# First layer of a graph network: sum gathered rows of x in three bfloat16 parts, multiply each finished bucket by w1

## The chip, the cores and the metric

The kernel runs on one core of a Trainium2 chip. The metric is device time in microseconds of one execution; lower is better.

## The reference

Two graph layers, each followed by a residual and a layer norm, on 6250 nodes of 256 features and 106250 edges that are sorted by destination:

```python
# first layer
w0_features = x @ w0
w1_features = x @ w1
neighbours = segment_sum(w1_features[src], dst, 6250)
x = layernorm(x + relu(w0_features + neighbours))
# second layer, 8 edge types r, 8 heads of 32
h_all = einsum('nf,rof->rno', x, W)
scores = leaky(h_all[type, src] . attn_src + h_all[type, dst] . attn_dst)
w = softmax of scores over the edges of one dst
x = layernorm(x + segment_sum(h_all[type, src] * w, dst, 6250))
```

## The kernel before, in words

All five engines run instruction lists that are written out by hand; semaphores join them. Nothing is scheduled by a planner: the order of the work is the order of the Python loops.

**Sort (start to about 251 us).** The first layer uses each edge in both directions of a sorted list, so the edges are first put in order of destination bucket. A bucket is 256 nodes, there are BK = 25 of them, and an order for the buckets is chosen by their number of columns; a column is 128 edges of one bucket, and there are 856 (COLS). VectorE does most of it: one-hot masks of buckets (L473, scalar_tensor_tensor over 896 elements, nine of thirteen; ScalarE makes the other four, L1396 to L1399), thirteen running counts (`tensor_tensor_scan`, L546, written to PSUM) each followed by a predicated copy (L538), and from about 101 us thirty steps that move the edges to their places through TensorE matmuls (L1644 `move`, L1656 `settle`; VectorE's L599 to L624). One multiplication on the way is GpSimd's: `jumps` (L1316).

**Products beside the sort.** Meanwhile SyncE loads x transposed (`load_chunk`, L1104), TensorE multiplies each tile of 128 nodes by w1 and w0 side by side (`products`, L1612, 128x512 float32), and ScalarE copies the halves out (`keep_products`): x·w1 through `y_two` (L1384) to the DRAM table `y_d` (L1128), x·w0 (L1385) into the running sums `sums0` in SBUF. Tiles 0 to 5 (EARLY) go before the counts, tiles up to Q_AT = 40 after, the rest between the thirty steps.

**First layer (251 to 1428 us).** For each group of four columns, `gather_columns` (L1303) issues four indirect DMAs on GpSimd, each fetching 128 rows of 256 float32 from `y_d` into a ring of five buffers (RING); ScalarE makes the one-hot selectors `sel0` (`column_one_hots`, L1461 and L1465); TensorE sums (`sum_columns`, L1687): two matmuls 128x128 by 128x256 for each column, one for each half of the bucket; VectorE adds the 512 sums of a column to its bucket (`add_columns`, L777). There are NG = 214 groups. `done_at(t)` is the group after which bucket t is complete, a new one about every 8.9 groups. A complete bucket goes through VectorE (`node_sums` L786 to L796: relu, residual, statistics), GpSimd (`inverse_deviation`, L1326), VectorE (`normalise`, L805), TensorE (`turn_nodes`, L1726, transposes), ScalarE (`copy_nodes`, L1491) and then ten units of the second layer's table (`table_unit` L1737 and L1740, `copy_unit` L1503 to L1512, stored to `ha_d`). turn_at and unit_at say how many groups after done_at these stand. The tables of the second layer's edges are made in the first groups as well (the AT table; GpSimd's L1311 gathers 7 times 128 rows of 512 float32).

**Drain (1428 to 1489 us).** After the last gather the last buckets (22, 23, 24) still go through those stages, and GpSimd waits for the last store to `ha_d`.

**Second layer (from 1489 us)**: 880 gathers from `ha_d` (L1348) with the score and softmax work; then a short tail. Neither is touched, except that a row of indices `tile_row` now shares its buffer with `bucket_row`.

SyncE's loads for the first layer's buckets and for W stand in one queue: W's transpose `WT` comes after the products and the edge rows, and TensorE's list waits for it (`t.wait_ge(wT_in, 16)`) once ahead of group 0.

Of the kernel before, what the change touches and what calls it, by code (L numbers as in the profile page):

```python
# [5 lines left out]
P = 128  # L6
# [15 lines left out]
def graph_layers(nc, x, xT, src, dst, etype, w0, w1, W, WT, attn_src, attn_dst, out):  # L22
# [58 lines left out]
    EARLY = 6  # L81
    GOES_AT, Q_AT = 35, 40
    assert WW <= P and COLS <= KR and OH <= 512 and E <= P * KR and NP_ * 512 < 2 ** 24
    assert WW * HC < HIGH and HIGH * HIGH <= 2 ** 24 and KR < HIGH and NPAIR <= 16
    assert OH % 4 == 0 and OH <= 512 and NT - 1 - Q_AT <= NBT // 2 and 2 * NBT * PP <= P
# [6 lines left out]
    y_d = dram("y_d", [NP_, D], F32)  # L92
# [9 lines left out]
    with ExitStack() as ctx:  # L102
# [7 lines left out]
        RW = 25600  # L110
# [14 lines left out]
        tile_row = sb("tile_row", [1, KP], I32)  # L125
        bucket_row = sb("bucket_row", [1, KR], I32)
        wab = sb("wab", [P, DC, 2 * RH], F32)
# [49 lines left out]
        def view16(base, at, *shape):  # L177
# [22 lines left out]
        cells_i = view(region, RW - COLS, COLS).bitcast(I32)  # L200
        assert GA + NPAIR * KR // 2 <= RW - COLS
        win = [view16(region, GA, TB, WW)] + [view16(region, GA + TB * WW // 2 * n, TB // 2, WW, 2) for n in range(1, 4)]
        at = [view16(region, GA + 2 * TB * WW + TB * HC * n, 2, TB // 2, HC, 2) for n in range(3)]
        iota_h = view16(region, RW - COLS - COLS // 2, COLS)
        assert GA + 2 * TB * WW + 3 * TB * HC + KR <= RW - COLS - COLS // 2
# [3 lines left out]
        w01 = view(edge_z, o, DC, 2 * D); o += 2 * DC * D  # L209
        x_t = [view(edge_z, o + 2 * DC * P * n, DC, 2 * P) for n in range(2)]; o += 4 * DC * P  # L210
        y_two = [view(edge_z, o + 2 * D * n, 2, D) for n in range(2)]; o += 4 * D
        misc = view(nodes, NT * D, NT * H)
        assert o <= 4864
# [47 lines left out]
        assert 2 * R * AW <= 4 * D * RING  # L261
        rows0 = [view(region, o + 4 * D * n, 4, D) for n in range(RING)]; o += 4 * D * RING
        sel0 = [view(region, o + 4 * SPAN * n, 4, SPAN) for n in range(SEL)]; o += 4 * SPAN * SEL
# [3 lines left out]
        xn = [view(edge_z, o + 2 * D * h, 2, D) for h in range(2)]; o += 4 * D  # L267
        tmp = [view(edge_z, o + 2 * D * h, 2, D) for h in range(2)]; o += 4 * D
# [60 lines left out]
        names = """pads_set edges_in acol_in w_in iotas setup sort_ps sort_in y_ps y_done y_kept bt_made masked counted v_made  # L329
            goes_made cells_made scans summed wp_made split_made grids_made at_made at_filled win_v win_a moved halves_made s_near s_made  # L330
# [59 lines left out]
        def y_tile_at(k):  # L390

            return Q_AT + k // 2 + 1 if k % 2 and Q_AT + k // 2 + 1 < NT else None
# [19 lines left out]
        def turn_at(t):  # L412

            return done_at(t) + (9 if t < BK - 1 else 13)
# [4 lines left out]
        def unit_at(t, k):  # L419

            return done_at(t) + (10 if t < BK - 1 else 19) + 9 * k // 10
# [1464 lines left out]
```

## Time and profile before

| what | us |
|---|---|
| median of 3 runs | 2759.0 (2754.98 to 2760.86) |
| profiled execution, its own time | 2753.04 |
| its span, first to last instruction | 2751.2 |
| TensorE, VectorE, ScalarE, GpSimd busy | 2309.0, 1940.0, 1637.1, 1841.7 |
| granted TensorE clock, mean | 0.902 |

The span is 1.8 us shorter than the execution's time. In the rows below PE is TensorE, PEld its weight loads, DVE VectorE, ACT ScalarE and POOL GpSimd. A busy share is a mean over four stages with different limits, so the rows are taken stage by stage.

### The profile page before, as it was taken

Reading aid. Unit: us, or ns where it says so; the run is one execution under the profiler, and the core shown is the slowest. Engines: PE = TensorE matmul, PEld = TensorE weight load, DVE = VectorE, ACT = ScalarE, POOL = GpSimd, SP = SyncE. Lnnn points to the kernel's source line nnn. Section 1 sums busy time; section 2 is a strip of 40 time slices with the busy share of each in tenths; the row PEclk is TensorE's granted clock in tenths of the full one; section 3 lists DMA queues with packets and bytes.
Section 4 is the critical chain, followed back from the end, with each engine's and each line's share of the span. In section 5 each row is a group of like instructions: output and inputs, shape, how many; then the busy total and the mean of one; then the engine's idle time right before and its main releaser. Section 6 shows DMA issues by size and latency. Waiting matters only on the chain. (4 is left out here: it accounts for less than half of the span.)

```text
span 2751.2 us, 38107 instructions
## 1 busy us (share of the span) xinstructions
PE 2309.0 (84%) x9936; PEld 1645.4 (60%) x9936; DVE 1940.0 (71%) x4273; ACT 1637.1 (60%) x3465; POOL 1841.7 (67%) x1875
## 2 busy tenths in 40 slices
PE   8796788999999999999987677777778878787775
PEld 3364666677777777777764555555555555555541
DVE  9895576555555555555552688888888888888887
ACT  4563455566666666666654566666666666666643
POOL 1002677777777777777762777777777777777735
PEclk9797899999999999999998698889888887889888
DMA  5202346764444444444464444554454445454535
GB/s 158 62 22 86 109 133 140 224 195 160 154 161 152 161 148 147 158 153 163 153 137 160 138 138 138 142 146 138 138 144 145 138 138 149 139 139 138 143 90 159
DMA packets 177777, 387.53 MB, mean 141 GB/s; under 512 B 42669, under 2 KB 106867, under 8 KB 171042
## 3 DMA queue, kind: packets, MB, share of 16 engines
q0 software_dynamic: 83888, 233.09, 30.4%
q1 hardware_dynamic: 86626, 99.05, 12.0%
q10 hardware_dynamic: 7056, 52.99, 4.9%
q8 instruction: 86, 1.41, 0.2%
q14 instruction: 121, 0.99, 0.1%
HBM read 302.96 MB, written 82.03 MB: 140 GB/s over the span
## 5 line engine op out<-in xcount | busy, mean ns | idle before, releaser
L1303 POOL DMA_INDIRECT region<-y_d,edge_z x856 | 875.2, 1022 | 472.1 <-issue 235.1
L1348 POOL DMA_INDIRECT region<-ha_d,idx_t x880 | 892.5, 1014 | 310.8 <-issue 228.9
L777 DVE TENSOR_TENSOR nodes<-ps,nodes 128x512 f32 x856 | 591.7, 691 | 501.8 <-PE ps L1687 384.7
L1687 PE MATMUL ps<-region 128*128 128x256 f32 x3424 | 795.0, 385 | 75.4 <-DMA region<-y_d,edge_z 22.9
L1687 PEld LDWEIGHTS ps<-region 128*128 128x128 f32 x3424 | 651.2, 193 | 250.6 <-issue 122.6
L1803 PE MATMUL ps<-region 128*128 128x264 f32 x1760 | 623.6, 485 | 160.0 <-DVE nodes L895 118.9
L1803 PEld LDWEIGHTS ps<-region 128*128 128x128 f32 x1760 | 350.9, 226 | 358.0 <-DVE nodes L895 239.4
L895 DVE TENSOR_TENSOR nodes<-ps,nodes 128x264 f32 x880 | 372.2, 423 | 54.2 <-DVE nodes L895 43.5
L1461 ACT ACTIVATE region<-iota_n,edge_z 128x256 f32<-128x256 f32 x856 | 364.7, 499 | 52.9 <-PE ps L1687 48.9
L1737 PE MATMUL ps<-region,edge_z 128*128 128x512 f32 x784 | 363.0, 592 | 4.0 <-ACT edge_z L1491 2.7
L1503 ACT COPY region<-ps 128x512 f32<-128x512 f32 x196 | 114.6, 586 | 341.6 <-PE ps L1737 290.8
L1786 PEld LDWEIGHTS ps<-edge_z,region 128*128 128x128 f32 x1760 | 258.5, 219 | 66.6 <-issue 51.6
L1556 ACT ACTIVATE region<-region,ones 128x512 f32<-128x512 f32 x220 | 158.8, 722 | 233.0 <-PE ps L1803 227.8
L1786 PE MATMUL ps<-edge_z,region 128*128 x1760 | 262.5, 300 | 28.9 <-issue 19.1
L1549 ACT ACTIVATE region<-iota_row,local_t 128x128 f32<-128x128 f32 x880 | 277.6, 386 | 0.0
L884 DVE TENSOR_TENSOR region<-region,ps 128x1024 f32<-128x1024 f32 x220 | 265.1, 1205 | 0.0
L1465 ACT ACTIVATE region<-region,ones 128x1024 f32<-128x1024 f32 x214 | 246.0, 1150 | 7.0
L1737 PEld LDWEIGHTS ps<-region,edge_z 128*128 128x128 f32 x784 | 146.9, 189 | 125.3 <-issue 114.0
L1542 ACT ACTIVATE region<-region,part 128x512 f32<-128x512 bf16 x220 | 155.4, 706 | 22.8 <-PE ps L1786 14.9
L1545 ACT ACTIVATE region<-region,ones 128x512 f32<-128x512 f32 x220 | 158.8, 722 | 7.1
L938 DVE TENSOR_TENSOR region<-region 128x128 f32<-128x128 f32 x55 | 16.1, 293 | 156.4 <-DMA region<-ha_d,idx_t 156.4
L1820 PE MATMUL ps<-ident,region 128*128 128x128 f32 x55 | 25.1, 457 | 93.7 <-DVE region L940 93.7
(265 smaller groups left out, 1857.6 us busy)
## 6 DMA issues: line engine op xcount, KB each, us to landing
ha_d<-region ACTq DMA_DIRECT2D x49, 1056.0 KB
region<-near_d SPq DMA_DIRECT2D x55, 512.0 KB, 5.4
region<-ha_d,idx_t POOLq DMA_INDIRECT x880, 2.9
region<-y_d,edge_z POOLq DMA_INDIRECT x856, 2.9
edge_z<-level_d SPq DMA_DIRECT2D x55, 136.0 KB, 3.7
kl_d<-region SPq DMA_DIRECT2D x8, 903.0 KB
edge_z<-kl_d SPq DMA_DIRECT2D x55, 129.0 KB, 2.7
y_d<-edge_z SPq DMA_DIRECT2D x25, 256.0 KB, 3.2
```

Source lines behind the costliest of these rows:

```text
L777: v.tensor_tensor(into, ps[:, u, :], into, ALU.add).then_inc(added0, 1)
L884: v.tensor_tensor(rows[s][:, 4 * q:4 * q + 4, 0:D].rearrange("p u (h d) -> p u h d", h=H), rows[s][:, 4 * q:4 * q + 4, 0:D].rearrange("p u ...
L895: v.tensor_tensor(acc[:, ds(tile * AW, AW)], ps[:, u, 0:AW], acc[:, ds(tile * AW, AW)], ALU.add).then_inc(added, 1)
L1303: g.indirect_dma_start(rows0[c % RING][:, u, :], None, y_d, bass.IndirectOffsetOnAxis(ap=y_idx[:, k:k + 1], axis=0), bounds_check=node_bou ...
L1348: g.indirect_dma_start(rows[s][:, k, :], None, ha_rows, bass.IndirectOffsetOnAxis(ap=idx_t[:, B * b + k:B * b + k + 1], axis=0), bounds_ch ...
L1461: last = a.activation(sel0[c % SEL][:, u, :], iota_n[:, :], ACT.Abs, bias=y_local[:, 4 * c + u:4 * c + u + 1], scale=-1.0)
L1465: a.activation(sel0[c % SEL].rearrange("p u n -> p (u n)"), sel0[c % SEL].rearrange("p u n -> p (u n)"), ACT.Relu, bias=ones[:, 0:1], scal ...
L1549: last = a.activation(apart[q % 2][:, u, :], iota_row[:, :], ACT.Abs, bias=local_t[:, ds(B * b + 4 * q + u, 1)], scale=-1.0)
L1687: mm = t.matmul(ps[:, u, h * D:(h + 1) * D], lhsT=sel0[c % SEL][:, u, h * P:(h + 1) * P], rhs=rows0[c % RING][:, u, :], start=True, stop=True)
L1737: mm = t.matmul(ps[:, 4 + n % 2, :], lhsT=xts[par][:, h, c, :], rhs=wT_sb[:, c, 512 * q:512 * q + 512], start=(c == 0), stop=(c == DC - 1))
L1786: mm = t.matmul(ps[:, 5 + q // 2, at_col:at_col + RH], lhsT=st[q][:, u, :], rhs=b_sb[:, ds(tile[u] * RH, RH)], start=True, stop=True)
L1803: t.matmul(ps[:, u, 0:AW], lhsT=sel[q][:, u, :], rhs=rows[b % 4][:, 4 * q + u, :], start=True, stop=True).then_inc(segs, 1)
```

## The change

**The table of products goes.** No `products`, no `keep_products`, no `y_d`. Instead each chunk of x (12 of 128 partitions by 4 rows of 256, and one of 106 rows) is split into three bfloat16 parts whose sum is x: ScalarE rounds (`round_high`), GpSimd subtracts in place (`take_high`), ScalarE rounds the rest (`round_rest`), GpSimd subtracts again into the third part (`take_mid`), SyncE stores the three parts (`store_chunk`) to `x3_d`. Four chunks are in flight (HELD). GpSimd then sets `sums0` to zero (128x12800).

**The gather** fetches rows of 768 bfloat16 instead of 256 float32, and a column is summed by six bfloat16 matmuls (three parts, two halves), accumulated in PSUM; the selectors are bfloat16.

**A finished bucket** has four stages more ahead of `node_sums`: `turn_sums` (TensorE, 4 transposes), `copy_sums` (ScalarE), `node_products` (TensorE: 4 matmuls of x by w0 and 4 of the sums by w1, into one bank of PSUM), and SyncE loads the bucket's columns of x transposed (`load_columns`). `turn_at` and `unit_at` are one group earlier (three for bucket 23 and 24). TensorE's wait for WT moves from ahead of group 0 to the first table unit.

```diff
+            def take_high(k):
+                p, t = chunk_of(k)
+                g.wait_ge(x_high, k + 1)
+                g.tensor_tensor(x_in[k % HELD][p, t, :], x_in[k % HELD][p, t, :], x_parts[k % HELD][p, t, 0, :],
+                                ALU.subtract).then_inc(x_rest, 1)
+
+            def take_mid(k):
+                p, t = chunk_of(k)
+                g.wait_ge(x_mid, k + 1)
+                g.tensor_tensor(x_parts[k % HELD][p, t, 2, :], x_in[k % HELD][p, t, :], x_parts[k % HELD][p, t, 1, :],
+                                ALU.subtract).then_inc(x_low, 1)
+
+            take_high(0)
+            for k in range(CHUNKS):
+                if k + 1 < CHUNKS:
+                    take_high(k + 1)
+                take_mid(k)
+                if k == JUMPS_AT:
+                    g.wait_ge(goes_made, 1)
+                    g.tensor_tensor(jumps, ...)
+            for n in range(HELD):
+                g.wait_ge(x_stored[n], 16 * chunks_in(n))
+            g.memset(sums0, 0.0).then_inc(sums_zero, 1)
...
-            def keep_products(tile):
+            def round_high(k):
+                a.wait_ge(x_loaded[k % HELD], 16 * (k // HELD + 1))
+                if k >= HELD:
+                    a.wait_ge(x_stored[k % HELD], 16 * (k // HELD))
+                a.copy(x_parts[k % HELD][p, t, 0, :], x_in[k % HELD][p, t, :]).then_inc(x_high, 1)
+            def round_rest(k):
+                a.wait_ge(x_rest, k + 1)
+                a.copy(x_parts[k % HELD][p, t, 1, :], x_in[k % HELD][p, t, :]).then_inc(x_mid, 1)
...
-                    g.indirect_dma_start(rows0[c % RING][:, u, :], None, y_d,
+                    g.indirect_dma_start(rows0[c % RING][:, u, :], None, x3_d,
...
-                        mm = t.matmul(ps[:, u, h * D:(h + 1) * D], lhsT=sel0[c % SEL][:, u, h * P:(h + 1) * P],
-                                      rhs=rows0[c % RING][:, u, :], start=True, stop=True)
+                        for k in range(PARTS):
+                            mm = t.matmul(ps[:, u, h * D:(h + 1) * D], lhsT=sel0[c % SEL][:, u, h * P:(h + 1) * P],
+                                          rhs=rows0[c % RING][:, u, k * D:(k + 1) * D], start=(k == 0), stop=(k == PARTS - 1))
...
+            def node_products(job):
+                for h in range(2):
+                    for c in range(DC):
+                        t.matmul(ps[:, 7, h * D:(h + 1) * D], lhsT=x_t[par][:, c, h * P:(h + 1) * P],
+                                 rhs=w01[:, c, D:2 * D], start=(c == 0), stop=False)
+                    for c in range(DC):
+                        mm = t.matmul(ps[:, 7, h * D:(h + 1) * D], lhsT=sums_t[par][:, h, c, :],
+                                      rhs=w01[:, c, 0:D], start=False, stop=(c == DC - 1))
...
-            t.wait_ge(wT_in, 16)
```

Where the instructions moved, GpSimd's list from its start to the first gather. `nodes` is the buffer that holds the chunks of x and their parts, `region` holds `jumps`. Before:

```order
L1292 ISA
L1292 IOTA region 128x896
L1293 IOTA nodes 128x1
L1316 TENSOR_TENSOR region<-region 128x2600
L1303 DMA region<-y_d,edge_z 128x256 x64
```

Now, to the first of the alternating subtractions:

```order
L1333 ISA
L1333 IOTA region 128x896
L1334 IOTA nodes 128x1
L1359 TENSOR_TENSOR nodes<-nodes 128x1024 x2
L1365 TENSOR_TENSOR nodes<-nodes 128x4x256
L1359 TENSOR_TENSOR nodes<-nodes 128x1024
```

GpSimd did one multiplication before the first gather. Now L1359 and L1365 go on in turn to 24 subtractions of 1024 elements and two of 256; `jumps` (now L1375) stands behind the sixth L1365, and the memset of `sums0` and the gathers behind the last.

TensorE's list around the last sum of columns, where the drain begins. Before, L1687 is that sum, L1726 `turn_nodes`, L1737 and L1740 table units:

```order
L1737 MATMUL ps<-region,edge_z 128x512 x2
L1687 MATMUL ps<-region 128x256 x8
L1740 MATMUL ps<-wab,edge_z 128x128 x2
L1726 MATMUL ps<-ident,edge_z 128x128 x4
L1737 MATMUL ps<-region,edge_z 128x512 x8
```

Now, L1740 is the sum, L1823 and L1826 are units, L1782 `turn_sums`, L1794 and L1797 `node_products`:

```order
L1740 MATMUL ps<-region 128x256 x24
L1823 MATMUL ps<-region,edge_z 128x512 x6
L1782 MATMUL ps<-ident,nodes 128x128 x4
L1823 MATMUL ps<-region,edge_z 128x512 x2
L1794 MATMUL ps<-region,edge_z 128x256 x2
L1797 MATMUL ps<-region,edge_z 128x256 x2
```

The products of bucket 23, and behind them those of bucket 24, stand between the units of bucket 22; the transposes L1726 of bucket 22 moved ahead of the last sum.

## Rows read from the trace of the kernel before

**Rows 1.** Windows of the stages: busy us (instructions) of each engine, clock, DMA share.
```profile
core 0: us, PE busy (x) PEld busy (x) DVE busy (x) ACT busy (x) POOL busy (x), PEclk, DMA share, GB/s
0.00:251.00 251.00, 203.91 (x1317) 119.93 (x1317) 220.72 (x359) 131.97 (x357) 8.32 (x8) 0.87 0.23 66
251.00:1428.00 1177.00, 1101.12 (x4449) 821.46 (x4450) 676.60 (x1106) 721.28 (x1365) 898.87 (x886) 0.97 0.51 158
1428.00:1489.00 61.00, 50.68 (x160) 26.93 (x158) 24.00 (x32) 19.32 (x43) 2.31 (x3) 0.98 0.41 131
```
**Rows 2.** Line L1303, the gathers: idle time of GpSimd before them, by releaser.
```profile
  issue: 235.1, 777
  DVE edge_z L661: 196.8, 1
  PE ps L1687: 40.2, 78
```
**Rows 3.** Groups of GpSimd, 251 to 1489 us: busy us, mean ns | idle us before.
```profile
L1326 POOL TENSOR_TENSOR rstd<-veps,minus_half 128x2 f32<-128x2 f32 x25 | 18.8, 750 | 16.5 <-DVE veps L796 16.0
L1311 POOL DMA_INDIRECT region<-edge_rows_d,nodes x7 | 7.1, 1012 | 2.1 <-issue 2.1
```
**Rows 4.** Timeline of GpSimd: start, us, instruction [idle before <-releaser].
```profile
47.01 6.97 POOL L1316 TENSOR_TENSOR region<-region 128x2600 f32<-128x2600 f32 x1 [45.20 <-DVE region L551]
297.35 1.01 POOL L1303 DMA_INDIRECT region<-y_d,edge_z  x1 [9.74 <-PE ps L1687]
298.67 1.01 POOL L1303 DMA_INDIRECT region<-y_d,edge_z  x1 [0.30 <-issue]
318.26 1.01 POOL L1303 DMA_INDIRECT region<-y_d,edge_z  x1 [5.13 <-PE ps L1687]
```
**Rows 5.** Timeline of VectorE around GpSimd's multiplication, and its memset in the drain.
```profile
46.84 2.09 DVE L546 TENSOR_TENSOR_SCAN ps<-ones,region 128x896 f32<-128x896 f32 x1
48.84 1.17 DVE L538 COPY_PREDICATED region<-region,ps 128x896 f32<-128x896 int16 x1
50.04 5.83 DVE L546 TENSOR_TENSOR_SCAN ps<-ones,region 128x896 f32<-128x896 f32 x1
...
1449.22 11.06 DVE L846 MEMSET nodes<- 128x13200 f32 x1 [2.70 <-DMA x_d<-edge_z]
```
**Rows 6.** Groups of VectorE in the sort, 0 to 251 us.
```profile
L546 DVE TENSOR_TENSOR_SCAN ps<-ones,region 128x896 f32<-128x896 f32 x13 | 30.7, 2368 | 0.2
L617 DVE TENSOR_SCALAR region<-region 104x856 f16<-104x856 f16 x60 | 23.7, 436 | 10.6 <-PE ps L1656 10.2
L624 DVE TENSOR_TENSOR region<-ps,region 104x512 f16<-104x512 f32 x30 | 20.5, 682 | 5.4 <-PE ps L1644 5.4
L473 DVE SCALAR_TENSOR_TENSOR region<-region 128x896 bf16<-128x896 f32 x9 | 9.2, 1089 | 0.0
L465 DVE CAST region<-region 128x896 f32<-128x896 int32 x1 | 0.6, 628 | 0.0
```
**Rows 7.** ScalarE, page, costliest groups: one pass over 1024 elements.
```profile
L1465 ACT ACTIVATE region<-region,ones 128x1024 f32<-128x1024 f32 x214 | 246.0, 1150 | 7.0
```
**Rows 8.** Timeline of TensorE: a product and a `settle` in the sort, then the later stages.
```profile
119.02 3.10 PE L1612 MATMUL ps<-edge_z 128*128 128x512 f32 x4
...
232.18 1.63 PE L1656 MATMUL ps<-region 104*128 104x428 f16 x8
...
269.96 9.68 PE L1687 MATMUL ps<-region 128*128 128x256 f32 x32 [21.07 <-DMA region<-WT_in]
...
1430.55 3.73 PE L1687 MATMUL ps<-region 128*128 128x256 f32 x16 [1.20 <-DMA region<-y_d,edge_z]
...
1439.56 0.61 PE L1740 MATMUL ps<-wab,edge_z 128*128 128x128 f32 x4
1440.01 0.60 PE L1726 MATMUL ps<-ident,edge_z 128*128 128x128 f32 x4
...
1450.00 7.11 PE L1737 MATMUL ps<-region,edge_z 128*128 128x512 f32 x16 [0.32 <-ACT region L1503]
```

More of the change, by code:

```diff
@@ L349, in graph_layers @@
         xt_in = [sem(f"xt_in{h}") for h in range(2)]
-        y_stored = [sem(f"y_stored{h}") for h in range(2)]
         x1_kept = [sem(f"x1_kept{h}") for h in range(2)]
@@ L808, in _ @@
             pad_rows()
-            v.wait_ge(jobs_made, 1)
-            job_regs = [v.alloc_register(f"sum_job{k}") for k in range(BK - 1)]
-            v.load(job_regs, job_row[0:1, 0:BK - 1])
-            jobs = [v.snap(r, min_val=0, max_val=BK - 2) for r in job_regs] + [BK - 1]
             for g in range(NG + LATE):
@@ L1400, in _ @@
                              accum_out=cnt_all[:, t:t + 1]).then_inc(counted, 1)
-                keep_products(k + 1)
-            for tile in range(NPAIR - MASKED + 1, EARLY):
-                keep_products(tile)
+                split_chunk(k)
             a.wait_ge(sort_ps, PS["v"])
@@ L1408, in _ @@
                        ps[:, 4 + n, 0:(blocks.stop - blocks.start) * P].rearrange("p (b t) -> p b t", t=P)).then_inc(sort_in, 1)
-            for tile in range(EARLY, Q_AT + 1):
-                keep_products(tile)
-                if tile == GOES_AT:
+            for k in range(NPAIR - MASKED, CHUNKS):
+                split_chunk(k)
+                if k == GOES_AT:
                     a.wait_ge(sort_ps, PS["goes"])
@@ L1442, in _ @@
                     windows_of(ahead, TBG // 2 * (k % 4), TBG // 2 * (k % 4) + TBG // 2)
-                if y_tile_at(k) is not None:
-                    keep_products(y_tile_at(k))
                 if k == 2:
@@ L1601, in turn_rows @@
                 return mm
-            t.wait_ge(w_in, 32)
-            def products(tile):
-                it, h = tile // 2, tile % 2
-                if h == 0:
-                    t.wait_ge(xt_in[it % 2], 16 * (it // 2 + 1))
-                if tile >= 2:
-                    t.wait_ge(y_done, tile - 1)
-                for c in range(DC):
-                    mm = t.matmul(ps[:, tile % 2, :], lhsT=x_t[it % 2][:, c, h * P:(h + 1) * P], rhs=w01[:, c, :],
-                                  start=(c == 0), stop=(c == DC - 1))
-                mm.then_inc(y_ps, 1)
-            for tile in range(EARLY):
-                products(tile)
             t.wait_ge(counted, NPAIR - MASKED + 1)
@@ L1624, in _ @@
             turn_rows(v_row, 4).then_inc(sort_ps, 1)
-            for tile in range(EARLY, Q_AT + 1):
-                products(tile)
-                if tile == GOES_AT:
-                    t.wait_ge(goes_made, 3)
-                    t.transpose(ps[0:WW, 7, P:2 * P], goes_row, ident[:, :]).then_inc(sort_ps, 1)
+            t.wait_ge(goes_made, 3)
+            t.transpose(ps[0:WW, 7, P:2 * P], goes_row, ident[:, :]).then_inc(sort_ps, 1)
             t.wait_ge(summed, NPAIR + 2)
@@ L1664, in _ @@
                     settle(k - 1)
-                if y_tile_at(k) is not None:
-                    products(y_tile_at(k))
                 if k == 1:
@@ L1755, in _ @@
                 for job in range(BK):
+                    if c == sums_at(job):
+                        turn_sums(job)
+                    if c == sums_at(job) + 1:
+                        node_products(job)
                     if c == turn_at(job):
```

226 lines of the change are left out of this document (147 added, 79 removed).

## The prediction

> **What bounds the kernel now.** I read the windows of the stages first, then for each stage the engine that is never idle in it.
>
> In the **sort** that is VectorE: 220.7 of 251 us busy [rows 1]. GpSimd stands idle for 196.8 us there, until the sorted indices are out [rows 2]. So whatever lengthens VectorE's chain delays the first gather one for one.
>
> In the **first layer** it is GpSimd. A gather takes 1.01 us and the next starts 1.32 us after it (298.67 against 297.35) [rows 4]; 856 of them are 1130 us of the stage's 1177 [rows 1]. Of the rest, 26 us are the 25 small powers (18.8 us) and the seven gathers of table rows (7.1) [rows 3]. Only 40.2 us in 78 pieces is waiting for TensorE [rows 2], and most pieces are as long as the pause that any gather has (235.1/777 = 0.30 us), so the true loss is 40.2 - 78 x 0.30 = **16.8 us**, nearly all in two places, 9.74 and 5.13 us [rows 4]. TensorE looks just as busy, 1101 of 1177 us, and DMA has half its share free (0.51) [rows 1].
>
> In the **drain** it is TensorE, 50.7 of 61 us [rows 1].
>
> **The change, part by part, on the path.** All sums are made against the profiled execution's 2753.0 us.
>
> *1. Subtractions beside the sort.* GpSimd gets 24 subtractions of 1024 elements and two of 256. The nearest row is its multiplication of 2600 elements, 6.97 us from 47.01 [rows 4]. A scan on VectorE ran from 46.84 to 48.93 [rows 5]. If GpSimd began only behind it, the work took 53.98 - 48.93 = 5.05 us, 1.94 ns an element; if it began at once, 2.68 ns. A subtraction is thus 2.0 or 2.7 us, and I take 2.0, because the other engine's row says who waited: the next scan, started at 50.04, took 5.83 us instead of 2.09 and ended 1.9 us after the multiplication did, so it began when that was over. The predicated copy between them took its usual 1.17 [rows 5, 6]. A scan has two operands in SBUF (ones and masks), the copy has its data in PSUM. **I conclude that a VectorE instruction with two SBUF operands and a GpSimd operation of this kind exclude each other.**
>
> The masks (L473, 1.09 us for 896 elements, two SBUF operands) are the scan's kind. The casts (0.63 us) have one operand but take 0.70 ns an element where the masks take 1.2, so I count them as using the second path too; if they do not, 7 us less.
>
> Stepping the hand-written lists with 2.0 us a subtraction, 1.15 us for a ScalarE rounding [rows 7] and the rows of VectorE: (a) from 14 us on, nine subtractions alternate with the nine masks, and each holds the next mask for most of its 2.0 us: 16 us. (b) Three fall among short operations, many with no second SBUF operand: 3.5 us. (c) The other twelve run beside the thirteen scans. Where one starts as a scan ends, the copy (1.17) goes on beside it and the next scan waits 0.85 us: nine of them, 7.6 us. Three stand ahead of casts or of another two-operand instruction at 2.0: 6 us. Sum 16 + 3.5 + 7.6 + 6 = **+33 us**. Lower bound, if scans alone are held: 12 x 0.85 = 10. Upper, at 2.7 us each: 33 + 24 x 0.74 = 51. I take 33. The subtractions end some 115 us into the kernel, well before the gathers need them, so the split itself is hidden; the price is VectorE's.
>
> The page SBUF — State Buffer of the Trainium skill, section Who interferes with whom, says the same of two-SBUF-input instructions against a GpSimd instruction that reads SBUF, and of casts that use both ports; by it the sum is the 33. It speaks against placing this work on GpSimd beside a VectorE-bound sort, and the scan's row agrees with it. The page GPSIMD Engine Reference, section 3.1, gives 4497 ns for a float32 tensor_tensor of 2048; an estimate from that page is 2.3 us a subtraction, by which the term would be about 40.
>
> *2. Zeroing `sums0`.* 12800 elements on GpSimd; VectorE's memset of 13200 took 11.1 us [rows 5]. It comes once the last part is stored, when VectorE still runs scans, and 130 us before the first gather. No row shows a GpSimd memset beside VectorE: between 0 and +11; I take 0, as GpSimd's idle 196.8 us covers it and the copy's row shows that operations without a second operand pass.
>
> *3. Products leave the sort.* In the thirty steps VectorE waits 10.2 + 5.4 us for TensorE [rows 6], partly behind products of up to 3.1 us [rows 8]. The rest is TensorE's own moves, which stay. Bounds 0 and -15.6; I take half, **-8 us**.
>
> *4. Start of the first layer.* TensorE's first sum is held to 269.96 by WT [rows 8]; that wait moves away, and TensorE starts some 10 us earlier, as soon as rows and selectors are there. GpSimd's two long waits at 297 and 318 follow from that late start, so they go: **-16.5 us**, the most that GpSimd's row allows. Bounds: 0 and -16.8.
>
> *5. Rows of 1536 bytes.* A gather of 2048-byte rows took 1012 ns, like one of 1024 [rows 3]: 0 on GpSimd. Gathered bytes grow by half; DMA's share would go from 0.51 to at most 0.75. 0 to +20 us in case landings get late; I take 0.
>
> *6. TensorE's steady load.* For each bucket (8.9 groups, 8.9 x 4 x 1.32 = 47.0 us of GpSimd) it had sums of 8.9 x 3.73 = 33.2 us, units 2 x (7.11 + 0.61) = 15.4, transposes 0.6 [rows 8]: 49.2, a little over what the overlapped records really cost. Now: bfloat16 columns are priced by the f16 row, 1.63/8 for 428 columns, 0.122 us for 256; 24 in a group make 2.9, 26.0 for 8.9 groups; units 15.4; 16 product instructions at 3.73/16 make 3.7; two sets of transposes 1.2: 46.3. That is 2.9 less than by the same pricing before, so GpSimd stays the bound: 0.
>
> *7. Drain.* Behind the last sum TensorE gets two sets of products (2 x 3.7) and two of `turn_sums` (1.2), loses one set of transposes and the wait for its copy (0.6 + 1.5), has a last sum of 2.9 instead of 3.7 us and one hop of about 1 that nothing covers: 8.6 - 2.1 - 0.8 + 1 = 6.7, of which some 2.5 replaces waits between units: **+4 us**; bounds 0 and +9.
>
> **Sum:** 33 - 8 - 16.5 + 4 = +12.5, so 2765.5 on the profiled execution. That one lies 6 us under the median of the runs shown, so the forecast is **2772 us**.
>
> **Rivals.** *A: only scans are held.* Then term 1 is 10, VectorE loses little, and 10 - 8 - 16.5 + 4 = -10.5: 2749 us, faster. For it: the scan's is the only stall the rows show. Against: the masks have the same two operands. It decides in the masks, at 14 to 24 us: if they still end by 26, it is so. *B: subtractions cost 2.7 us.* Term 1 is 51: 2790. For it: 6.97 us is what the row says; against: the scan that was running when it began. *C: the first layer gets a new bound* (late landings, or bfloat16 matmuls no quicker than f16 rows say): 10 to 20 us more, some 2790. *D: the change does not do what it says*: if a 256-column bfloat16 matmul costs what a float32 pass does (3.73/16 = 0.23), a group is 24 x 0.23 = 5.6 us and a bucket 5.6 x 8.9 + 20.3 = 70 against 47: over 500 us slower. The f16 row speaks against it, at 0.20 us for 428 columns.
>
> **How the numbers follow.** The forecast 0.48, A 0.25, B 0.15, C 0.10, D 0.02. About 0.2% (5.5 us) is what a measurement here can tell from no change. The forecast's own terms spread from 2757 (casts not held, all of term 3) to 2785 (nothing of term 3, a drain of +9), so it gives some 0.10 to "same"; A reaches into it too. Faster 0.25, same 0.13, slower 0.62. The range goes from A with all of term 3 gained, 2742, to B with most of the memset's 11 us, 2798.
>
> **What would show it.** Right: masks that end near 40 us instead of 24; scans of 2.8 to 4 us where a subtraction of about 2.0 us runs; the first gather near 275 instead of 251; GpSimd hardly waiting for TensorE between the first and the last gather, about 1160 us apart; a drain of about 65 us. Wrong: masks back to back beside subtractions (A); subtractions of 2.7 us (B); gathers that wait for TensorE in mid-stage, or sums that wait for rows (C, D); or a second layer that changes, which no step touches.

## The result, and the profile after

The changed kernel takes **2789.3 us** (median of 4 runs, 2787.9 to 2790.5) against 2758.0 (4 runs, one more than ahead of the prediction, 2755.0 to 2760.9): ratio 1.0109, 95% interval 1.0096 to 1.0123, or 31 us slower. The profiled execution took 2790.5 us with a span of 2788.7, that is 37.5 more than the span of before. (The profiled execution of before lies 5 us under its median, this one 1 above; that is the rest.)

Windows of the stages after, columns as in [rows 1]:

```profile
core 0: us, PE busy (x) PEld busy (x) DVE busy (x) ACT busy (x) POOL busy (x), PEclk, DMA share, GB/s
0.00:280.00 280.00, 120.54 (x1117) 86.48 (x1117) 258.27 (x357) 124.80 (x283) 88.68 (x34) 0.91 0.21 70
280.00:1456.00 1176.00, 1061.52 (x6599) 754.85 (x6599) 675.42 (x1106) 726.39 (x1387) 900.00 (x886) 0.95 0.68 211
1456.00:1523.00 67.00, 57.77 (x223) 33.69 (x220) 25.28 (x34) 21.41 (x47) 1.42 (x3) 0.95 0.41 134
1523.00:2788.00 1265.00, 946.70 (x4012) 674.73 (x4012) 1018.52 (x2779) 764.54 (x1700) 936.30 (x980) 0.84 0.49 140
```

The sort holds almost all of it: 280 us instead of 251, with VectorE busy for 258 instead of 221 on nearly the same instructions (357 and 359). The first layer is as long as before. Measured between the starts of fixed instructions, in us (the rank phase is the running counts and what follows them up to a cast, L569 before and L593 now; then the first and the last gather of the first layer, and the first of the second):

| stretch | before | after | difference |
|---|---|---|---|
| start to the end of the rank phase | 94.1 | 130.3 | +36.2 |
| to the first gather | 156.7 | 149.9 | -6.8 |
| first to last gather | 1175.9 | 1174.8 | -1.1 |
| drain | 61.9 | 68.4 | +6.5 |
| second layer | 1262.6 | 1265.3 | +2.7 |

The last line is scatter: in the kernels below, none of which touches the second layer, it takes 1261.8 to 1266.0. Each figure is from one traced execution, and the others scatter too. From the rank phase to the first gather the code of before took 153.9 to 157.9 us in three executions, that of after 146.8 to 156.0 in seven (means 156.2 and 150.5). The drain took 61.6 to 61.9 in the former three, and 65.9 to 69.9 in all ten executions that have the change's four stages.

**The sort.** Groups of VectorE, 0 to 131 us, which answer to [rows 6], and of GpSimd, 0 to 281 us:

```profile
L570 DVE TENSOR_TENSOR_SCAN ps<-ones,region 128x896 f32<-128x896 f32 x13 | 36.6, 2823 | 0.2
L562 DVE COPY_PREDICATED region<-region,ps 128x896 f32<-128x896 int16 x13 | 14.9, 1145 | 0.1
L497 DVE SCALAR_TENSOR_TENSOR region<-region 128x896 bf16<-128x896 f32 x9 | 22.5, 2559 | 0.0
L590 DVE CAST region<-region 128x896 int32<-128x896 f32 x1 | 4.3, 4305 | 0.0
```

```profile
L1359 POOL TENSOR_TENSOR nodes<-nodes 128x1024 f32<-128x1024 f32 x12 | 34.7, 2893 | 7.6 <-ACT nodes L1444 7.6
L1365 POOL TENSOR_TENSOR nodes<-nodes 128x1024 bf16<-128x1024 f32 x12 | 33.8, 2820 | 12.5 <-ACT nodes L1449 12.5
```

A mask takes 2.56 us instead of 1.09, a scan 2.82 instead of 2.37; the predicated copy keeps its 1.15. VectorE's idle time up to the end of the rank phase does not grow (4.6 us, against 6.8 before): the wait for the other engine is inside the instruction's own record. So it is on GpSimd's side. Its timeline, and VectorE's, with the cast of before to compare:

```profile
19.52 2.97 POOL L1365 TENSOR_TENSOR nodes<-nodes 128x1024 bf16<-128x1024 f32 x1
...
85.77 3.84 POOL L1365 TENSOR_TENSOR nodes<-nodes 128x1024 bf16<-128x1024 f32 x1
89.57 2.12 POOL L1359 TENSOR_TENSOR nodes<-nodes 128x1024 f32<-128x1024 f32 x1
...
117.25 10.77 POOL L1379 MEMSET nodes<- 128x12800 f32 x1 [6.84 <-DMA x_d<-nodes]
```

```profile
15.14 2.43 DVE L495 CAST region<-region 128x896 f32<-128x896 int32 x1
...
20.44 3.00 DVE L497 SCALAR_TENSOR_TENSOR region<-region 128x896 bf16<-128x896 f32 x1
...
91.73 3.95 DVE L570 TENSOR_TENSOR_SCAN ps<-ones,region 128x896 f32<-128x896 f32 x1
...
119.75 2.09 DVE L570 TENSOR_TENSOR_SCAN ps<-ones,region 128x896 f32<-128x896 f32 x1
121.75 2.41 DVE L562 COPY_PREDICATED region<-region,ps 128x896 f32<-128x896 int16 x2
124.19 4.30 DVE L590 CAST region<-region 128x896 int32<-128x896 f32 x1
```

```profile
91.70 0.63 DVE L566 CAST region<-region 128x896 int32<-128x896 f32 x1
```

Beside seven of the nine masks the two engines alternate, with a period of 2.93 us on both: one mask (the next starts 1.01 us later where nothing holds it) and one subtraction (some 1.9). A subtraction that nothing holds takes 2.12; one that meets a scan reads 3.84. A cast is held as well (2.43 us at 15.14, 0.63 by itself). The memset, which reads nothing, lets a scan pass (2.09), but the cast behind it, L590, ends only 0.5 us after the memset does at 128.0. So the 36.2 us of the rank phase are 32.5 ahead of L590 (124.19 against 91.70) and 3.7 in it (4.30 against 0.63).

**The first layer.** GpSimd's first gather and its long waits, to be set against [rows 4]:

```profile
280.19 1.30 POOL L1344 DMA_INDIRECT region<-x_d,edge_z  x1 [152.18 <-DVE edge_z L685]
321.77 1.01 POOL L1344 DMA_INDIRECT region<-x_d,edge_z  x1 [4.65 <-PE ps L1740]
342.73 1.01 POOL L1344 DMA_INDIRECT region<-x_d,edge_z  x1 [5.08 <-PE ps L1740]
...
379.36 0.73 POOL L1386 TENSOR_TENSOR rstd<-veps,minus_half 128x2 f32<-128x2 f32 x1 [4.77 <-DVE veps L821]
```

The wait of 9.74 has halved, that of 5.13 is still there, and a new one of 4.77 stands behind them: the power (`inverse_deviation`) keeps its place seven groups after `done_at`, but `node_sums`, on which it waits, went from one group after `done_at` to three. TensorE's rows of the same stretch and of the drain, one of ScalarE, and three of TensorE before (two of the first layer, one of the drain) say where the rest comes from:

```profile
291.11 4.59 PE L1740 MATMUL ps<-region 128*128 128x256 bf16 x24 [12.21 <-DMA region<-x_d,edge_z]
297.62 4.48 PE L1740 MATMUL ps<-region 128*128 128x256 bf16 x24 [1.92 <-DMA region<-x_d,edge_z]
301.93 2.75 PE L1750 MATMUL ps<-nodes,edge_z 128*128 128x16 f32 x24
...
305.76 5.28 PE L1750 MATMUL ps<-nodes,edge_z 128*128 128x16 f32 x24
...
316.22 11.02 PE L1740 MATMUL ps<-region 128*128 128x256 bf16 x72 [3.46 <-issue]
...
1465.26 4.47 PE L1740 MATMUL ps<-region 128*128 128x256 bf16 x24 [2.80 <-DMA region<-x_d,edge_z]
```

```profile
312.79 0.21 ACT L1538 COPY wab<-ps 128x64 f32<-128x64 f32 x1 [22.92 <-PE ps L1750]
```

```profile
279.47 2.75 PE L1697 MATMUL ps<-nodes,edge_z 128*128 128x16 f32 x24
...
282.96 3.16 PE L1697 MATMUL ps<-nodes,edge_z 128*128 128x16 f32 x24
...
1435.99 3.73 PE L1687 MATMUL ps<-region 128*128 128x256 f32 x16
```

L1750 are the **small weights**: W times the attention vectors, 32 matmuls (64 records) that TensorE does once, behind the second sum of columns. ScalarE copies their result behind its second selectors, so it waits 22.92 us for them and starts no third selectors until 313.2; the third sum comes at 316.22. The block is in the kernel before at the same place (L1697, 279.47 to 287.82 us there). Its two halves are of equal length in work, yet the second takes 5.28 us against 2.75: the granted clock fell from its upper to its lower level meanwhile, and its mean over the block is 0.64, against 0.85 in the kernel before.

### The profile page after: what moved, and what is told of

Its sections match the earlier page's. It is cut to its first block and busy times, and to the rows that moved or that the text cites. A ratio compares the mean times of both kernels' runs of the same rounds, so it can differ in the third digit from the quotient of the medians.

```text
span 2788.7 us, 42188 instructions
## 1 busy us (share of the span) xinstructions
PE 2186.5 (78%) x11948; PEld 1549.8 (56%) x11948; DVE 1977.5 (71%) x4273; ACT 1637.2 (59%) x3416; POOL 1926.4 (69%) x1902
## 5 line engine op out<-in xcount | busy, mean ns | idle before, releaser
L1344 POOL DMA_INDIRECT region<-x_d,edge_z x856 | 876.2, 1024 | 419.0 <-issue 238.1
L1740 PE MATMUL ps<-region 128*128 128x256 bf16 x5136 | 655.8, 285 | 111.9 <-DMA region<-x_d,edge_z 63.8
L1892 PE MATMUL ps<-region 128*128 128x264 f32 x1760 | 617.4, 481 | 160.6 <-DVE nodes L916 120.3
L1740 PEld LDWEIGHTS ps<-region 128*128 128x128 bf16 x5136 | 513.4, 102 | 289.2 <-issue 112.2
L1892 PEld LDWEIGHTS ps<-region 128*128 128x128 f32 x1760 | 347.0, 224 | 356.3 <-DVE nodes L916 238.9
L1527 ACT ACTIVATE region<-iota_n,edge_z 128x256 bf16<-128x256 f32 x856 | 364.8, 500 | 40.1 <-PE ps L1740 34.0
L1823 PE MATMUL ps<-region,edge_z 128*128 128x512 f32 x784 | 365.2, 594 | 3.1 <-ACT region L1575 3.1
L1875 PEld LDWEIGHTS ps<-edge_z,region 128*128 128x128 f32 x1760 | 261.2, 221 | 66.9 <-issue 52.0
L1531 ACT ACTIVATE region<-region,ones 128x1024 bf16<-128x1024 bf16 x214 | 245.8, 1148 | 7.0
L1823 PEld LDWEIGHTS ps<-region,edge_z 128*128 128x128 f32 x784 | 137.0, 191 | 117.7 <-issue 115.4
```

What stands on the lines that cost most here:

```text
L1344: g.indirect_dma_start(rows0[c % RING][:, u, :], None, x3_d, bass.IndirectOffsetOnAxis(ap=y_idx[:, k:k + 1], axis=0), bounds_check=node_bo ...
L1527: last = a.activation(sel0[c % SEL][:, u, :], iota_n[:, :], ACT.Abs, bias=y_local[:, 4 * c + u:4 * c + u + 1], scale=-1.0)
L1531: a.activation(sel0[c % SEL].rearrange("p u n -> p (u n)"), sel0[c % SEL].rearrange("p u n -> p (u n)"), ACT.Relu, bias=ones[:, 0:1], scal ...
L1740: mm = t.matmul(ps[:, u, h * D:(h + 1) * D], lhsT=sel0[c % SEL][:, u, h * P:(h + 1) * P], rhs=rows0[c % RING][:, u, k * D:(k + 1) * D], st ...
L1823: mm = t.matmul(ps[:, 4 + n % 2, :], lhsT=xts[par][:, h, c, :], rhs=wT_sb[:, c, 512 * q:512 * q + 512], start=(c == 0), stop=(c == DC - 1))
L1875: mm = t.matmul(ps[:, 5 + q // 2, at_col:at_col + RH], lhsT=st[q][:, u, :], rhs=b_sb[:, ds(tile[u] * RH, RH)], start=True, stop=True)
```

## The experiments

Each kernel was timed against the kernel before on the same chip. All ratios are to that kernel; the changed kernel's is 1.0109 (1.0096 to 1.0123), and 0.001 is 2.8 us.

**What the subtractions cost** (`e1_narrow`)

```diff
+            for n in range(HELD):
+                g.memset(x_parts[n][:, :, 2, :], 0.0)
-                g.tensor_tensor(x_in[..][p, t, :], x_in[..][p, t, :], x_parts[..][p, t, 0, :], ...
+                g.tensor_tensor(x_in[..][p, t, 0:16], x_in[..][p, t, 0:16], x_parts[..][p, t, 0, 0:16], ...
```

(and the same in `take_mid`)

> Left out: GpSimd's subtractions work on 16 of every 256 columns of x (the third parts are set to zero once at the start), so the second and third parts are wrong. All 26 subtractions, their waits, ScalarE's roundings and SyncE's loads and stores stay. Theory: VectorE's chain is 36.2 us later than before (130.95 against 94.78) because each subtraction of 2.1 us holds VectorE's two-operand instructions. Then masks end by about 27 us instead of 40, scans take 2.1 to 2.6 us again, the chain ends at about 97 to 100, and the whole gains 30 to 34 us (about 2757). Rival: the chain is late because of ScalarE, which rounds between its own masks, or of the loads of x; then masks still end near 40 and the time stays within 5 us of 2789.

Measured: 2753.7 us, ratio 0.9990 (0.9980 to 1.0000). The rank phase ends at 96.8 instead of 130.3, the first gather comes at 245.2. VectorE's groups of this run, 0 to 131 us:

```profile
L570 DVE TENSOR_TENSOR_SCAN ps<-ones,region 128x896 f32<-128x896 f32 x13 | 30.6, 2363 | 0.2
...
L497 DVE SCALAR_TENSOR_TENSOR region<-region 128x896 bf16<-128x896 f32 x9 | 9.7, 1138 | 0.0
```

The cast L590 of this run:

```profile
94.06 0.95 DVE L590 CAST region<-region 128x896 int32<-128x896 f32 x1
```

ScalarE's roundings and SyncE's transfers are all still there, so the rival is out: the width of GpSimd's operands alone moves the end of the chain by 33.5 us. Of these, 30.1 lie ahead of the cast (124.19 against 94.06). The other 3.4 are the cast's: in this run the chain reaches it just as the memset ends (94.5), and it takes 0.95.

**The memset** (`e3_small_memset`)

```diff
+            g.memset(sums0[:, HELD * ROWS * D * 5 // 2:], 0.0)
             take_high(0)
...
-            g.memset(sums0, 0.0).then_inc(sums_zero, 1)
+            g.memset(sums0[:, 0:64], 0.0).then_inc(sums_zero, 1)
```

> Left out: sums0 is not zeroed but for its first 64 elements at the old place and its last 2560 at the very start, so the first layer's sums start from what the buffer held. Theory: the memset of 10.8 us holds VectorE's casts (one took 4.30 us instead of 0.63 until the memset's end), so without it the chain from the rank phase to the first gather is 3.7 us shorter: first gather at about 276.5, time about 2785. Rival: the casts only moved the wait, and VectorE then waits for TensorE or ScalarE in the thirty steps: first gather stays at 280, time within 1 us of 2789.

Measured: 2783.0 us, ratio 1.0092 (1.0074 to 1.0110); the interval overlaps that of the changed kernel, so the time decides nothing. In the trace the cast is back to its own length and the rank phase ends 2.6 us earlier (127.7):

```profile
125.26 0.63 DVE L590 CAST region<-region 128x896 int32<-128x896 f32 x1
```

The first gather still came at 281.6: the thirty steps took 4 us longer in this execution, at a clock of 0.73 to 0.86 in their later windows. The chain had reached the cast 1.1 us later than in the changed kernel, so the rank phase gained 2.6 and not the 3.7 that the cast gave back. So the hold is shown, and its price at the first gather is not.

**The wait for WT** (`e2_wt_ahead`, `e6_before_wt_moved`): put back in the changed kernel, moved alone in the kernel before.

```diff
+            t.wait_ge(wT_in, 16)
             unit = 0
```

> TensorE's wait for WT is put back ahead of group 0. Theory A (as predicted): the wait is what makes GpSimd lose its two long waits of 9.7 and 5.1 us in the first layer, and something new took the gain; then putting it back costs 12 to 17 us (2801 to 2806). Theory B: GpSimd's long waits follow from the small weights L1750, which hold TensorE for 11 us and ScalarE's selectors for 23 us just behind the second sum; the wait for WT only shifts when that block begins, by some 8 us less the slower clock of the block. Then it costs 4 to 6 us (2793 to 2795) and GpSimd waits 9 to 10 us near 327 and still 5 us some 20 us later. Theory C: the wait is hidden: within 2 us of 2789.

Measured: 2797.3 us, ratio 1.0149 (1.0133 to 1.0165), some 11 us more than the change by the two ratios; first to last gather 1182.6 against 1174.8. GpSimd waits 10.91 us at 327 and 4.19 at 347. Between B and A by the time, at B by the trace.

```diff
-            t.wait_ge(wT_in, 16)
             unit = 0
...
+                if n == 0:
+                    t.wait_ge(wT_in, 16)
```

> The kernel before with one part of the change alone: TensorE's wait for WT goes from ahead of group 0 to the first table unit. The prediction took 16.5 us for it. Theory B, from the run that put the wait back (first layer 1182.6 against 1174.8): 6 to 9 us, so 2748 to 2751, with the wait of 9.7 us at 297 about halved and the one of 5.1 us still there. Rival: in the kernel before it hides a wait that the change has removed, and gives 14 us or more (2743 or less).

Measured: 2749.5 us, ratio 0.9966 (0.9953 to 0.9978), 9.4 us faster; first to last gather 1171.6 against 1176.0, with waits of 2.91, 4.87 and 2.89. So the wait is worth 4 to 8 us in the first layer of either kernel and 9 to 11 by the ratios, and not the 16.5 that were forecast. The rival's 14 is out.

**The small weights** (`e4_weights_early`, `e5_weights_ahead`)

```diff
             for k in range(NBT):
                 move(k)
                 if k:
                     settle(k - 1)
+                if 10 <= k < 10 + DC * R:
+                    small_weights(k - 10)
```

> The small weights (L1750 and ScalarE's copies L1538 and L1539) leave the first layer: TensorE does them in 16 pieces beside steps 10 to 25 of the sort, ScalarE copies them ahead of its first selectors. Theory B: then neither TensorE nor ScalarE stops behind the second sum, GpSimd's wait at 321 (4.65 us) goes, the first wait of a gather comes later and is shorter, and the time falls by 4 to 9 us (2780 to 2785). Theory A or C: the waits come from late rows (WT and the edge rows share the DMA queues in the first 20 us) or from VectorE's table work, so GpSimd waits as long as before and the time stays within 2 us of 2789. If the pieces delay the thirty steps, the first gather comes after 280.

Measured: 2782.9 us, ratio 1.0102 (1.0087 to 1.0118): no measurable gain. But the parts moved far: first to last gather 1161.7 instead of 1174.8, and from the rank phase to the first gather 159.6 instead of 149.9. VectorE's waits in the steps, of the changed kernel and of this one:

```profile
DVE region L641 <- PE ps L1712: 3.8, 4, 1.6
```

```profile
DVE region L641 <- PE ps L1711: 13.7, 10, 2.4
```

TensorE's pieces, 0.6 us each, were not free there: VectorE waits for `settle` ten times instead of four. So the block goes where TensorE idles, in the 12 us before the first rows land:

```diff
+            small_weights()
             unit = 0
             for c in range(NG + LATE):
                 if c < NG:
                     sum_columns(c)
-                if c == AT["wab"]:
-                    small_weights()
...
-                if c == AT["wab"]:
+                if c == SEL - 1:
                     small_weights()
```

> In the changed kernel, TensorE does the small weights in one block between the last settle of the sort and the first sum, where it waited 12 us for the first rows; ScalarE copies them behind its third selectors instead of its second. In the run that did them beside the thirty steps the first layer fell from 1174.8 to 1161.7 us but the steps grew by 10. Theory B: the block at the start is what cost the first layer its 13 us and the steps only lost TensorE time; here both are saved: first layer about 1162, steps as in the changed kernel (147 to 150), time 2772 to 2777. Rival: the gain came from a warm TensorE clock or from gathers that started later, not from the block; then the first layer stays at 1172 to 1176 and the time at 2785 to 2789.

Measured: 2775.3 us, ratio 1.0067 (1.0054 to 1.0080), 11.6 us faster than the change; first to last gather 1160.6, the steps as they were (148.9). TensorE's rows:

```profile
277.69 2.79 PE L1750 MATMUL ps<-nodes,edge_z 128*128 128x16 f32 x24
...
282.03 5.28 PE L1750 MATMUL ps<-nodes,edge_z 128*128 128x16 f32 x24
...
289.60 4.89 PE L1740 MATMUL ps<-region 128*128 128x256 bf16 x24 [0.58 <-DMA region<-x_d,edge_z]
296.49 10.12 PE L1740 MATMUL ps<-region 128*128 128x256 bf16 x72 [2.01 <-DMA region<-x_d,edge_z]
```

The third sum follows the second without a break, and GpSimd's waits for TensorE, of the changed kernel and of this one, become the pause that any gather has:

```profile
POOL region L1344 <- PE ps L1740: 28.7, 66, 5.1
```

```profile
POOL region L1344 <- PE ps L1740: 16.7, 57, 0.3
```

The power's wait of 4.77 is gone too, though `node_sums` stands where the change put it; one of 3.45 us at 619 is the only wait of GpSimd over 0.8 us that is left in the stage. TensorE's block and ScalarE's copies moved together here, so which of the two held the third sum is not separated; nor did a run move the block and keep WT's wait. And the block fell to the lower clock level here as well (0.51 in the window from 280 to 290 us), straight behind the last `settle`, with no wait of TensorE in front of it.

**The wide rows** (`e10_one_part`, `e11_ahead_one_part`)

```diff
-                    g.indirect_dma_start(rows0[c % RING][:, u, :], None, x3_d, ...
+                    g.indirect_dma_start(rows0[c % RING][:, u, 0:D], None, x3_d, ...
...
-                                          rhs=rows0[c % RING][:, u, k * D:(k + 1) * D], ...
+                                          rhs=rows0[c % RING][:, u, 0:D], ...
```

> Left out: the changed kernel gathers only the first part of each row, 512 bytes instead of 1536, and sums that part three times, so the work of TensorE is the same and the output lacks two parts. Theory (wide rows are hidden, as predicted): the first layer stays at 1172 to 1177 us and the time at 2785 to 2790; only the drain, where the last sum waited 2.8 us for rows, gets 2 to 4 us shorter. Rival: late rows in the first 20 us (the first sum came 11 us after the first gather) are what keeps the first layer from gaining: then the first sum comes 2 us or more earlier and the first layer falls by 4 us or more.

Measured: 2775.5 us, ratio 1.0069 (1.0049 to 1.0090): 11 us faster, against the theory. First to last gather 1164.2. But the drain stayed at 68.3, and the first sum came only 1 us earlier (10.0 us after the first gather instead of 10.9), so the rival is not right as it was put either. What differs in this trace is the clock. TensorE's rows, and the window 300 to 310 us of the changed kernel and of this one:

```profile
290.39 5.15 PE L1740 MATMUL ps<-region 128*128 128x256 bf16 x24 [11.25 <-DMA region<-x_d,edge_z]
297.45 2.80 PE L1740 MATMUL ps<-region 128*128 128x256 bf16 x24 [1.90 <-DMA region<-x_d,edge_z]
300.09 2.75 PE L1750 MATMUL ps<-nodes,edge_z 128*128 128x16 f32 x24
...
303.58 3.53 PE L1750 MATMUL ps<-nodes,edge_z 128*128 128x16 f32 x24
...
312.27 10.05 PE L1740 MATMUL ps<-region 128*128 128x256 bf16 x72 [3.46 <-issue]
```

```profile
300.00:310.00 10.00, 10.00 (x64) 9.48 (x62) 2.05 (x3) 0.00 (x0) 7.60 (x8) 0.67 0.54 165
```

```profile
300.00:310.00 10.00, 8.81 (x67) 8.71 (x64) 1.41 (x3) 1.15 (x6) 7.56 (x9) 0.78 0.16 48
```

The second sum takes 2.80 us here and 4.48 there, the block of small weights 8.7 (mean clock 0.81) against 10.8 (0.64), and the third sum comes 4 us earlier. Whether the narrower rows brought the higher clock is not shown: the block took 8.35 to 11.2 us in the six kernels that keep it at its place with wide or float32 rows. And the third sum is not the whole gain. Of the 10.6 us of the stage, 6.2 are idle time of GpSimd (269.6 us between its instructions instead of 275.8) and 4.4 are its instructions' own records (894.3 instead of 898.7). The same edit on top of `e5_weights_ahead`:

> Left out: as in the run with one part, only the first 512 bytes of each row are gathered and summed three times; and the small weights stand ahead of the first sum, as in the run that took 2775.3 us. Theory: the wide rows cost the changed kernel 11 us only because they keep TensorE waiting and its clock low where the block of small weights holds up the first groups; without the block on that path the narrow rows gain little: first layer 1158 to 1162 us, time 2771 to 2776. Rival: wide rows cost about 10 us on their own, over the whole first layer (GpSimd's issues, late rows, VectorE's stages): then the first layer falls to about 1150 and the time to 2763 to 2767.

Measured: 2770.2 us, ratio 1.0043 (1.0029 to 1.0057); first to last gather 1157.0 against 1160.6. With the block out of the way the narrow rows give 3.6 us in the first layer instead of 10.6 (6.6 by the ratios, in intervals that overlap). Stage and time lie just under the theory's ranges and above the rival's. So 4 (by the ratios) to 7 (by the traces) of the 11 hang on the block, and 4 to 7 are the rows' own. Of the 3.6 in the layer, 2.1 are idle time of GpSimd (262.1 instead of 264.2), 1.6 its own records (894.7 instead of 896.3).

**Versions that beat both kernels** (`e7_before_weights_ahead`, `e8_split_on_tensor`, `e9_split_ahead`). The first is the kernel before with the WT wait moved (as above) and the small weights ahead of the first sum (as above), and nothing of the change's split.

> The kernel before with the wait for WT moved and the small weights ahead of the first sum, that is without the change's split and its four stages. Theory B: the first layer loses nothing to TensorE, 1160 to 1163 us instead of 1176, so 2741 to 2745. Rival: float32 sums of 3.7 us a group leave TensorE too little room in the first groups and GpSimd waits again: 1168 us or more, 2749 or more.

Measured: 2743.2 us, ratio 0.9942 (0.9929 to 0.9955); first to last gather 1164.1.

The second keeps the change, has the small weights ahead of the first sum, and takes the subtractions from GpSimd. TensorE forms x minus its parts in PSUM, ScalarE rounds from there and zeroes `sums0` (operands shortened):

```diff
-            def take_high(k): ...
-            def take_mid(k): ...
-            g.memset(sums0, 0.0).then_inc(sums_zero, 1)
+                    t.matmul(rest, lhsT=ident, rhs=x_in, start=True, stop=False)
+                    t.matmul(rest, lhsT=neg_ident, rhs=high, start=False, stop=True)
...
+                    t.matmul(rest, lhsT=ident, rhs=x_in, start=True, stop=False)
+                    t.matmul(rest, lhsT=neg_ident, rhs=high, start=False, stop=False)
+                    t.matmul(rest, lhsT=neg_ident, rhs=mid, start=False, stop=True)
...
+                    z = a.activation(sums0[:, at:at + n], ones[:, 0:1].to_broadcast([P, n]), ACT.Copy, scale=0.0)
```

> The changed kernel without GpSimd's subtractions: TensorE forms x minus its rounded parts in PSUM (identity and minus identity), ScalarE rounds from there, ScalarE zeroes the sums in 13 pieces beside steps 8 to 20, and the small weights stand ahead of the first sum. Theory (the price is VectorE's, held by GpSimd's two-operand work): masks end near 23 us, scans take 2.1 us, the rank phase ends near 95 to 100, the first gather comes at 242 to 250, the first layer takes about 1162: 2738 to 2748, faster than both kernels. Rival: what GpSimd no longer does, ScalarE and TensorE do late: the chain waits for ScalarE's copies or for TensorE's transposes behind the split, the rank phase ends at 105 or later, or the thirty steps take 155 or more: 2752 or more.

Measured: 2750.8 us, ratio 0.9965 (0.9953 to 0.9978). The rank phase ends at 93.0, earlier than in the kernel before, but the steps take 158.5 us, so the rival holds for them: two chunks were placed among them, and VectorE waits up to 6.2 us behind one for a `settle`. The third has all chunks ahead:

> The run with the split on TensorE and ScalarE, but all 13 chunks ahead of the transposes that the rank phase needs (93.7 us there; eleven chunks were done at 84, five us each), none in the thirty steps. Theory: the two chunks in the steps held VectorE for 6.2 us behind a settle, so from the end of the rank phase to the first gather it takes 149 to 153 us instead of 158.5, the rank phase ends at 93 to 95, and the time is 2742 to 2747. Rival: the steps are long because ScalarE's 13 pieces of zeroing or TensorE's clock hold them, not the chunks: then still 156 or more, and 2749 or more.

Measured: **2739.3 us**, ratio 0.9935 (0.9917 to 0.9953), 48 us under the change by the two ratios, of which 11.6 are the small weights' (`e5_weights_ahead`): rank phase to 94.2, steps 149.6, first layer 1165.5, drain 66.9. VectorE's groups are those of the kernel before again:

```profile
L583 DVE TENSOR_TENSOR_SCAN ps<-ones,region 128x896 f32<-128x896 f32 x13 | 30.7, 2368 | 0.2
...
L510 DVE SCALAR_TENSOR_TENSOR region<-region 128x896 bf16<-128x896 f32 x9 | 9.2, 1089 | 0.0
```

The interval of this kernel overlaps that of `e7_before_weights_ahead` (0.9929 to 0.9955), which has nothing of the split. So that the split pays, once WT and the small weights are out of the way, is not shown, even where it costs VectorE nothing.

## Why the prediction was right in sign and wrong in size

The sign was right and the time lies in the range, but the forecast of 2772 was 17 us too low: it is 13 us above the median that it had, and the kernel became 31 slower. On the profiled executions it is +12.5 against +37.5. By the prediction's own steps, in us:

| term | forecast | measured | shown by |
|---|---|---|---|
| 1 subtractions | +33 | +32.5 | 124.19 - 91.70, the two traces; 30.1 of it in `e1_narrow` |
| 2 zeroing `sums0` | 0 | +3.7 | 4.30 - 0.63, `e3_small_memset` (trace) |
| 3 products leave the steps | -8 | -6.8 | the two traces (-5.6 between the means) |
| 4 start of the first layer, 5 wide rows | -16.5 and 0 | -1.1 together | the two traces, `e2` to `e11` |
| 7 drain | +4 | +6.5 | the two traces |

Of the 25 us that are missing, 15.4 are in terms 4 and 5, and 2.7 are the second layer's scatter.

**Term 1 was right, for the reason given.** A two-operand instruction on VectorE and a two-operand one on GpSimd exclude each other, the masks too, and the casts are held as the prediction had counted them (2.43 us). Rival A (scans alone) falls with the masks, which end at 40.1 us, rival B with the subtraction of 2.12, and rival D with a group of 24 bfloat16 matmuls, which took 2.80 us in `e10_one_part` and not the 5.6 of that rival. The page SBUF — State Buffer of the Trainium skill, section Who interferes with whom, states an exclusive lock on a shared port pair; by that rule the term is the 33 again, and the period of 2.93 us on both engines agrees.

**Term 2** was put at nothing because "operations without a second operand pass". The scans did pass, the cast did not, although term 1 had counted casts as held. The same section lists casts among what can take both port pairs; this trace shows one held for 3.7 us by an instruction that only writes.

**Term 4 is the step that failed.** The prediction put GpSimd's two long waits down to TensorE's late start behind WT: "GpSimd's two long waits at 297 and 318 follow from that late start, so they go". TensorE did start 8.2 us earlier (10.9 us after the first gather instead of 19.1). But what delays the third sum is the block of small weights, which the prediction never looked at: its rows for TensorE end with the first sums and go on in the drain. The earlier start brought the end of that block from 37.0 to only 32.6 us after the first gather. The two sums ahead of it took 10.8 us instead of 9.5, with a wait for rows between them, and the block itself, at the lower clock, 10.8 instead of 8.35. Why the clock was lower is open. TensorE's wait in front of the sums is not shown to be the cause: the block took 8.35 us behind a wait of 21.1 (before) and 9.6 behind 24.0 (`e2_wt_ahead`), but 10.8 behind 12.2 (after) and 11.3 behind none (`e5_weights_ahead`).

So, of term 4, the wait of 9.74 lost 5.1 us. That of 5.13 stayed. It is in the kernels that keep the block where it was (5.04 in `e1_narrow`, 4.87 in `e6_before_wt_moved`) and gone in `e5_weights_ahead`, so it hangs on the block too. And 4.8 us came back as the power's wait for the later `node_sums`, which the kernel before does not have (its powers wait 0.5 us in all in the stage); this one too is gone in `e5_weights_ahead`, so it takes the block and the later `node_sums` together. The four new stages ahead of `node_sums` were known, and the prediction did not ask what GpSimd has in its list at the old place. 15.3 us less was to be had: without the block on the path the first layer is 1160.6, close to the "about 1160" that the prediction named, so the size was right and the cause was not. In the kernel before it is the same: 1171.6 with the WT wait moved alone, 1164.1 with the block moved as well.

**Term 5** was put at 0 by the row of a 2048-byte gather, which is nearly right for GpSimd's issue. It is wrong for the whole: narrow rows gave 11 us with the block in place (`e10_one_part`), and 4 to 7 with the block out of the way (`e11_ahead_one_part`). That the rows had a share in term 4 is shown by these two runs; that it went through TensorE's clock is not.

**Term 7** missed 2.5, which is within the scatter of the drain (65.9 to 69.9). In this trace the last sum was to take 2.9 us and took 4.47 at the lower clock, after a wait for its rows, and its start was 1.0 us later after the last gather (10.3 against 9.2). The kernels with narrow rows have a drain of 65.9 and 68.3, so the width of the rows is not shown to be the cause. What is left, 6.5 - 1.0 - 1.6, is near the 4 that were forecast for the added products and transposes. (`turn_at` of bucket 24 is five groups earlier, not three as the section on the change has it.)

Rival C (a new bound of 10 to 20 us in the first layer) gives nearly the measured time, but only in part by its mechanism. The wide rows did cost some 11 us here, but they set no new bound: in mid-stage GpSimd's longest wait is 1.24 us, against 1.89 before.

## What to carry to other kernels

A wait in a trace names the last event, not the cause: before a stall is credited to an edit, follow each engine that could hold the waiting one past the point that the edit removes, ScalarE's and GpSimd's lists included. Work put on an idle GpSimd is paid by VectorE if both read two operands from SBUF, and here by VectorE's casts as well; the same work on TensorE and ScalarE cost the sort nothing here. And a one-off block belongs where its engine is waiting anyway, rather than in small pieces beside a chain that has no slack.

## What was not expected

- A subtraction of 1024 elements reads 2.12, 2.97 or 3.84 us, alone, beside masks and beside scans: the record includes the wait for the other engine, and so does VectorE's (4.30 us for a cast of 0.63). No idle time shows it in any view.
- GpSimd's memset of 12800 elements (10.77 us) holds a one-operand cast but not a scan with two operands (2.09 us beside it).
- TensorE's granted clock was low over the first 40 us of the stage: 0.56, 0.67, 0.67 and 0.50 in the four windows of 10 us from 280; in `e10_one_part` it was 0.58, 0.74, 0.78 and 0.71. The small weights, one and the same block, took 8.35 us (before, clock 0.85) to 11.6 (`e8_split_on_tensor`; 11.3 in `e5_weights_ahead`, clock 0.61).
- With one and the same code the stretch of the thirty steps takes 146.8 us (`e2_wt_ahead`) to 156.0 (`e11_ahead_one_part`); in the longest the granted clock was 0.73 to 0.84 in its later windows, in the shortest 0.80 to 0.92.
